# Experts' rows by a scatter into slots, or by a slot-to-row map and a gather per tile

## What is computed

```python
x = x + conv_attention(_ln_c(x), ...)          # 256 tokens per image, 32 key/query channels
t = _to_tokens(x)                              # 2048 tokens of 64 channels
flat = _ln_t(t)
probs = softmax(flat @ router_w.T)             # 8 experts
topk_probs, topk_idx = top_k(probs, 2)         # gates: the two, normalised
h = silu(flat @ w1[e].T) * (flat @ w3[e].T)    # 682 hidden channels
out = sum over the two experts of gate * (h @ w2[e].T)
x = _from_tokens(t + out)
```

## Time and profile before

| | us |
|---|---|
| Three runs | 239.73, 239.23, 238.13 |
| Median | 239.23 |
| The profiled execution | 238.83 |
| Its span, first to last instruction | 237.1 |

### The profile page before, as it was taken

The page is one execution under the profiler, slowest core; times in us unless marked ns, Lnnn a source line. Parts: engine busy times, 40 slices in busy tenths (PEclk is TensorE's granted clock), DMA queues, the critical chain, the costliest instruction groups (busy, mean ns, idle before and its releaser), DMA issues.

```text
span 237.1 us, 4275 instructions
## 1 busy us (share of the span) xinstructions
PE 169.0 (71%) x1424; PEld 136.2 (57%) x1424; DVE 117.4 (50%) x418; ACT 80.2 (34%) x169; POOL 92.1 (39%) x116
## 2 busy tenths in 40 slices
PE   2647789797923000079999999999999999995040
PEld 2536779686813000056787778778777778773010
DVE  3687697579458600025445554455446544552050
ACT  2246344341000000035445544554444544540020
POOL 6232520205777777400044334433443334436300
PEclk9999555555555555559999999999999999999555
DMA  4999500000001000030055534555455500000143
GB/s 138 428 409 411 239 3 0 0 0 7 30 17 33 29 23 29 24 90 0 3 145 170 179 124 132 157 182 144 126 149 178 165 16 13 17 17 17 40 164 80
DMA packets 11928, 24.46 MB, mean 103 GB/s; under 512 B 2435, under 2 KB 6563, under 8 KB 11395
## 3 DMA queue, kind: packets, MB, share of 16 engines
q1 hardware_dynamic: 9410, 21.59, 27.7%
q0 software_dynamic: 2496, 2.59, 3.3%
HBM read 16.74 MB, written 7.44 MB: 102 GB/s over the span
## 4 chain that ended last, share of the span: by engine, by line
issue 37%; POOL 31%; DVE 11%; PE 11%; DMA 5%; ACT 3%; POOLq 1%; SPq 0%; ACTq 0%
POOL ys L323 18%; POOL xs L282 11%; PE bank L787 4%; DVE xn L461 2%; DVE kq_right L493 2%; PE bank L775 2%; DMA y_in<-ys 2%; PE bank L737 1%; POOL rstd L266 1%; DVE parts L452 1%; DVE kq_left L488 1%; DMA x_sb<-x_tok 1%; DMA xs<-rows,pos 1%; DMA ys<-y_out,y_row 1%; DVE neg_max L498 1%
## 5 line engine op out<-in xcount | busy, mean ns | idle before, releaser
L698 DVE TENSOR_TENSOR hid<-bank,act_sb 128x512 f32<-128x512 f32 x69 | 47.6, 690 | 55.9 <-ACT act_sb L415 55.9
L323 POOL DMA_INDIRECT ys<-y_out,y_row x46 | 44.0, 957 | 79.4 <-DVE y_out L705 72.1
L896 PE MATMUL bank<-x_cols,weights 64*128 64x256 f32 x276 | 69.3, 399 | 1.1 <-ACT x_cols L409 0.6
L898 PE MATMUL bank<-x_cols,weights 64*128 64x256 f32 x276 | 69.3, 399 | 0.0
L896 PEld LDWEIGHTS bank<-x_cols,weights 64*128 64x128 f32 x276 | 49.2, 191 | 14.4 <-ACT act_sb L415 4.8
L415 ACT ACTIVATE act_sb<-bank 128x512 f32<-128x512 f32 x69 | 41.3, 598 | 33.3 <-PE bank L896 33.3
L898 PEld LDWEIGHTS bank<-x_cols,weights 64*128 64x128 f32 x276 | 49.3, 191 | 0.0
L913 PE MATMUL bank<-hid,weights 128*64 128x128 f32 x552 | 35.2, 277 | 0.5 <-ACT y_cols L421 0.5
L282 POOL DMA_INDIRECT xs<-rows,pos x32 | 31.2, 976 | 9.7 <-issue 9.7
L913 PEld LDWEIGHTS bank<-hid,weights 128*64 128x64 f32 x552 | 29.7, 137 | 4.3 <-DVE hid L698 3.3
L881 PE MATMUL bank<-ident,x_pairs 128*128 128x128 f32 x46 | 10.4, 309 | 26.4 <-DVE x_pairs L688 26.4
(11 more groups left out here) (123 smaller groups left out, 197.5 us busy)
## 6 DMA issues: line engine op xcount, KB each, us to landing
weights<-experts SPq DMA_DIRECT2D x23, 576.0 KB, 4.1
xs<-zeros SPq DMA_DIRECT2D x4, 1056.0 KB, 8.8
x_in<-xs SPq DMA_DIRECT2D x23, 66.0 KB, 1.9
y_in<-ys SPq DMA_DIRECT2D x4, 256.0 KB, 4.1
ys<-y_out,y_row POOLq DMA_INDIRECT x46, 3.5
xs<-rows,pos POOLq DMA_INDIRECT x32, 2.2
out<-result SPq DMA_DIRECT2D x8, 64.0 KB, 2.1
x_sb<-x_tok SPq DMA_DIRECT2D x1, 384.0 KB, 3.6
```

The source lines that it names most:

```text
L323: nc.gpsimd.indirect_dma_start(ys, bass.IndirectOffsetOnAxis(ap=y_row[:, i, h:h + 1], axis=0), y_out[:, i % RING, h, :], None).then_inc(y_ ...
L698: nc.vector.tensor_tensor(hid[:, g % HRING, :], H3_BANK[g % 3][:], act_sb[:, g % 3, :], ALU.mult).then_inc(hid_done, 1)
L896: first_ = nc.tensor.matmul(H1_BANK[g % 2][:, dst], weights[0:C, i % WSLOTS, at:at + P], x_cols[0:C, i % 2, :], start=True, stop=True)
L898: second_ = nc.tensor.matmul(H3_BANK[g % 3][:, dst], weights[C:P, i % WSLOTS, at:at + P], x_cols[C:P, i % 2, :], start=True, stop=True)
```

## The change

`xs` is now one row of 65 numbers (channels and gate) for each (token, choice) pair, in token order: SP writes it from `rows` in four plain DMAs, and nothing is cleared. Instead of moving rows to slots, the kernel computes the map from slot to pair, `slots`: 128 lanes x 128 columns, slot = 128 x column + lane. For each of the eight (column of tokens, choice) groups j of a block, VectorE makes two one-hot matrices (`lane_hot`, `column_hot`, the second scaled by the pair's number) and TensorE adds their product up in PSUM (`find_slots`); `add_slots` sums over blocks. GpSimd gathers the rows of a tile by this map into `x_in` with two indirect DMAs per tile, five tiles before it scatters that tile's results. For the extras the map's columns are picked by a transpose and a matmul with `select` in the first two tiles of the loop. The ID is no longer read from `x_in`: `y_row` is set by two `copy_predicated` in all instead of 23. `pair_up` now waits for the 32 counts of two gathers.

The diff, cut to its core:

```diff
@@ SP
-            sp.wait_ge(zeros_made, 1)
-            for q in range(NBLK):
-                sp.dma_start(xs[...], zeros[:]).then_inc(xs_cleared, 16)
             for e in range(E):
                 sp.dma_start(weights[:, e, :], experts[e]).then_inc(w_loaded[e], 16)
-            sp.wait_ge(dispatched, 16 * TILES * K_TOP)
-            for i in range(E):
-                sp.dma_start(x_in[:, i, :, :], xs[...]).then_inc(x_in_loaded[i], 16)
+            for k in range(NBLK):
+                sp.wait_ge(tn_ready, k + 1)
+                sp.wait_ge(gates_ready, k + 1)
+                sp.dma_start(xs.rearrange("(p t k) c -> p t k c", t=TILES, k=K_TOP)[:, tiles(k), :, :],
+                             rows[:, tiles(k), :, :]).then_inc(rows_stored, 16)
             sp.wait_ge(table_ready, 1)
             for i in range(E, NT):
...
-                sp.wait_ge(gated, i - WSLOTS + 1)
-                sp.dma_start(x_in[:, s, :, :], xs[bass.ds(r, SLOT), :]...).then_inc(x_in_loaded[s], 16)
                 sp.wait_ge(hid_used, STEPS * (i - WSLOTS + 1))
@@ GpSimd
-            def scatter_rows(k):
...
+            def gather_rows(i):
+                s = i % WSLOTS
+                if i >= WSLOTS:
+                    pool.wait_ge(gated, i - WSLOTS + 1)
+                if i == E:
+                    pool.wait_ge(extra_rows_ready, 1)
+                for h in range(HALVES):
+                    at = CAP // P * i + h
+                    index = slots_i[:, at:at + 1] if i < E else extra_rows[:, i - E, h:h + 1]
+                    nc.gpsimd.indirect_dma_start(x_in[:, s, h, :], None, xs,
+                                                 bass.IndirectOffsetOnAxis(ap=index, axis=0)
+                                                 ).then_inc(x_in_loaded[s], 16)
...
+            for k in range(NBLK):
+                inverse_deviation(1, k)
+            pool.wait_ge(rows_stored, 16 * NBLK)
+            pool.wait_ge(slots_added, NBLK)
+            for i in range(AHEAD):
+                gather_rows(i)
             for i in range(NT):
+                if i + AHEAD < NT:
+                    gather_rows(i + AHEAD)
+                scatter_results(i)
@@ ACT, expert loop
+                if i == 1:
+                    act.wait_ge(slots_turned, 1)
+                    nc.scalar.copy(slots_t[:], R_BANK[:, 0:P]).then_inc(slots_t_ready, 1)
@@ VectorE, positions(k)
-                    nc.vector.tensor_reduce(pos[:, k, :]..., place[:], AX.X, ALU.add).then_inc(pos_ready, 1)
+                    chain(nc.vector.tensor_reduce(pos[:]..., place[:], AX.X, ALU.add))
+                chain(nc.vector.tensor_scalar(low_bits[:], pos[:], P - 1, None, ALU.bitwise_and))
+                nc.vector.tensor_copy(pos_lane[:], low_bits[:]).then_inc(dve_step, 1)
+                chain(nc.vector.tensor_tensor(pos_column[:], pos[:], low_bits[:], ALU.subtract))
+                if k >= 2:
+                    dve.wait_ge(slots_done, k - 1)
+                for j in range(TPB * K_TOP):
+                    nc.vector.tensor_scalar(lane_hot[:, k % 2, j, :], lane[:], pos_lane[:, j:j + 1], None, ALU.is_equal)
+                    t = TPB * k + j // K_TOP
+                    nc.vector.tensor_scalar(column_hot[:, k % 2, j, :], column[:], pos_column[:, j:j + 1],
+                                            row_id[:, t, j % K_TOP:j % K_TOP + 1], ALU.is_equal, ALU.mult
+                                            ).then_inc(hot_ready, 1)
+            def add_slots(k):
+                dve.wait_ge(slots_done, k + 1)
...
+                    nc.vector.tensor_tensor(slots[:], slots[:], found, ALU.add).then_inc(slots_added, 1)
+                else:
+                    nc.vector.tensor_tensor(slots_i[:], slots[:], found, ALU.add).then_inc(slots_added, 1)
+                    nc.vector.tensor_tensor(slots[:], slots[:], found, ALU.add).then_inc(slots_added, 1)
@@ VectorE, order
                     weigh(k - 2)
+                    if k >= 3:
+                        add_slots(k - 3)
                     positions(k - 2)
...
             choose(NBLK - 2)
+            add_slots(NBLK - 3)
             weigh(NBLK - 2)
             positions(NBLK - 2)
             choose(NBLK - 1)
             weigh(NBLK - 1)
+            add_slots(NBLK - 2)
             positions(NBLK - 1)
+            add_slots(NBLK - 1)
             tile_table()
+            nc.vector.copy_predicated(y_row[:, 0:E, :], keep[:, 0:E, :], slots_i[:]...).then_inc(y_row_ready, 1)
@@ VectorE, expert loop
-                nc.vector.copy_predicated(y_row[:, i, :], keep[:, i, :], x_in[:, slot, :, ID].bitcast(I32)
-                                          ).then_inc(y_row_ready, 1)
+                if i == 1:
+                    result_rows_of_extras()
@@ TensorE
             def rank(k):
...
-                    pe.wait_ge(rank_read, k)
+                    pe.wait_ge(slots_added, k)
+            def find_slots(k):
+                for j in range(TPB * K_TOP):
+                    pe.wait_ge(hot_ready, TPB * K_TOP * k + j + 1)
...
+                    ins = nc.tensor.matmul(K_BANK[:, 0:COLS], lane_hot[:, k % 2, j, :], column_hot[:, k % 2, j, :],
+                                           start=(j == 0), stop=(j == TPB * K_TOP - 1))
+                ins.then_inc(slots_done, 1)
...
                     similarity(BPB * (k + 1) + 1)
+                if k >= 3:
+                    find_slots(k - 3)
                 attend(BPB * k)
...
             transpose_t(NBLK - 1)
+            find_slots(NBLK - 3)
             rank(NBLK - 2)
             route(NBLK - 1)
+            find_slots(NBLK - 2)
             rank(NBLK - 1)
+            find_slots(NBLK - 1)
...
+                if i == 0:
+                    pe.wait_ge(slots_added, NBLK + 1)
+                    nc.tensor.transpose(R_BANK[:, 0:P], slots[:], ident[:]).then_inc(slots_turned, 1)
+                if i == 1:
+                    pe.wait_ge(slots_t_ready, 1)
+                    pe.wait_ge(select_ready, 1)
+                    nc.tensor.matmul(R_BANK[:, P:P + NX * HALVES], slots_t[:], select[:]..., start=True, stop=True
+                                     ).then_inc(selected, 1)
```

More of the change, by code:

```diff
@@ L271, in count_up, with scatter_results @@
                                allow_small_or_imprecise_dtypes=True).then_inc(tables_made, 1)
[L273 to L284 removed]
+            def gather_rows(i):
[10 more added lines that the diff above has]
+                                                 ).then_inc(x_in_loaded[s], 16)
+            def scatter_results(i):
+                pool.wait_ge(gated, i + 1)
+                pool.wait_ge(y_row_ready, 1 if i < E else 2)
+                for h in range(HALVES):
+                    nc.gpsimd.indirect_dma_start(
+                        ys, bass.IndirectOffsetOnAxis(ap=y_row[:, i, h:h + 1], axis=0),
+                        y_out[:, i % RING, h, :], None).then_inc(y_scattered[i % RING], 16)
             inverse_deviation(0, 0)
@@ L571, in positions @@
                 dve.wait_ge(rank_read, k + 1)
-                with nc.allow_low_precision(reason="row numbers: whole and below 2^24"):
-                    nc.vector.tensor_reduce(pos[:, k, :].rearrange("p (t c) -> p t c", c=K_TOP), place[:], AX.X,
-                                            ALU.add).then_inc(pos_ready, 1)
+                with nc.allow_low_precision(reason="slot numbers: whole and below 2^24"):
+                    chain(nc.vector.tensor_reduce(pos[:].rearrange("p (t c) -> p t c", c=K_TOP), place[:], AX.X,
+                                                  ALU.add))
+                chain(nc.vector.tensor_scalar(low_bits[:], pos[:], P - 1, None, ALU.bitwise_and))
+                nc.vector.tensor_copy(pos_lane[:], low_bits[:]).then_inc(dve_step, 1)
+                steps[0] += 1
+                chain(nc.vector.tensor_tensor(pos_column[:], pos[:], low_bits[:], ALU.subtract))
[9 more added lines that the diff above has]
+                dve.wait_ge(slots_done, k + 1)
+                found = K_BANK[:, 0:COLS]
+                if k >= 1:
+                    dve.wait_ge(slots_added, k)
+                if k == 0:
+                    nc.vector.tensor_copy(slots[:], found).then_inc(slots_added, 1)
+                elif k < NBLK - 1:
+                    nc.vector.tensor_tensor(slots[:], slots[:], found, ALU.add).then_inc(slots_added, 1)
+                else:
+                    nc.vector.tensor_tensor(slots_i[:], slots[:], found, ALU.add).then_inc(slots_added, 1)
+                    nc.vector.tensor_tensor(slots[:], slots[:], found, ALU.add).then_inc(slots_added, 1)
             def occupancy(part):
@@ L932, in _ @@
                     turn_x(i + 1)
+                if i == 0:
[4 more added lines that the diff above has]
+                    pe.wait_ge(select_ready, 1)
+                    nc.tensor.matmul(R_BANK[:, P:P + NX * HALVES], slots_t[:], select[:].rearrange("p i h -> p (i h)"),
+                                     start=True, stop=True).then_inc(selected, 1)
```

115 lines of the change are left out of this document (57 added, 58 removed).

## The result

| | us |
|---|---|
| Before, beside the changed kernel | 239.44 (238.13 to 239.73) |
| The changed kernel | 295.41 (294.08 to 296.26) |
| Ratio | 1.237, 95% interval 1.232 to 1.243 |
| Its profiled execution | 295.41, span 293.7 |

The forecast was 238.4 in a range of 235.4 to 243.0. It is wrong by 57 us. Both times are told, and both profiles are read.

The account below looks back on a forecast made before the run. Bounds: GpSimd's scatters before the loop, TensorE in the expert loop. 238.83 - 2.3 (earlier tile start) + 0.5 (TensorE's added steps) + 1.0 (loop stall) = 238.0, and 0.4 to the median: 238.4 us, range 235.4 to 243.0.

Parts of the forecast that it names:

- One-hots, 14.7 us for 64: Before the loop, VectorE makes 64 one-hots at 0.20 and 0.26 us, a pair 0.46, in all 14.7 us.
- The estimate of 0.127: Skill page's price of one one-hot on VectorE, 8.1 us for all 64; the forecast set it aside for measured rows.
- Map ready at 93.9, pair_up(0) at 99.2: Before the loop, VectorE's chain ends the map at 93.9; tiles start at 99.2 instead of 101.53: -2.3 us.
- Gathers ahead of the loop are hidden: GpSimd's first gathers run beside the table from 93.9 and land at 97.4, before pair_up(0) at 99.2: no cost.
- TensorE's +0.5: In the loop, TensorE gets one transpose (0.27) and one matmul of 30 columns (some 0.2): +0.5 us.
- The loop's +1.0: In the loop, four GpSimd DMAs a tile take 5.04 against 4.82 us; TensorE's stall from this lag: +1.0 us.
- a late gated passes into later gathers: In the loop, GpSimd's wait for a late gated delays the gathers two tiles on; no size in the sum.
- the 4.9 that bounded L: L is a gather's landing time in the loop, 2.1 to 4.9 us, median 3.5; 4.9 makes the stall 2.5.
- the prediction's own formula: TensorE's loop loss: 16 x 0.22 + L + 3.78 - 7.27 - 2.4, with L a gather's landing time; 1.1 us at 3.5.
- GpSimd sets the loop's pace: Rival: x_pairs copies slow GpSimd by 0.2 a tile above 5.04, loop stall 4.3, total 241.7 to 243.1; chance 0.24, at 242.4.
- The lock rule: Skill rule: each x_pairs copy shuts GpSimd out of writing descriptors, 5.33 us a tile, loop stall 5.7, total 243.1.
- no difference: Outcome that the change can't be told from the kernel before, within about 1% (236.8 to 241.6 us); chance 0.40.

Follow-up runs that it names:

- chip 4: The changed kernel with no edit, run again on another chip than the first runs, 10 executions: 240.88 us, against 238.8 for the kernel before.
- the first run: The changed kernel with no edit, in its first measurement, chip not known: 295.41 us, against 239.44 for the kernel before.
- the kernels made from it: The kernel before with dummy gathers, dummy scatters or a memset added behind the scatters of all or some tiles: 238.59 to 312.62 us.
- pauses: The changed kernel with memsets on GpSimd as pauses: one behind each pair of indirect DMAs 279.65 us, one behind each four 272.12 us.
- plain stores: The changed kernel with each tile's results stored by two plain DMAs instead of two scatters, output not right: 232.37 us.
- dummies in tiles 0 to 5: The kernel before with two more full scatters to a spare tensor behind each of tiles 0 to 5 only: 238.59 us.
- chips 12 and 6: Kernel before plus one scatter 240.84, a memset 242.33, two 16-row scatters 246.15; two full scatters in tiles 0 to 5 238.59, 17 to 22 246.75 us.
- chips 0, 8 and 13: Kernel before plus two DMAs a tile: gathers 300.5, full scatters 308.3 and again 307.15, scatters of 64 rows 285.05, of 96 rows 312.62 us.
- eight runs in two groups: Variants of both kernels with added, shortened, spaced or replaced GpSimd DMAs: four on chip 12, 232.37 to 246.15 us, four on chip 8, 272.12 to 312.62 us.

## Why the prediction was right or wrong

**Without the late signals** (chip 4) it can be judged by its own steps. The page of this profile, against the earlier trace rows, and the stage of the earlier trace rows:

```profile
PE   2647789787734924599999996989998999997031
...
POOL 3232620201020003771677775777777777564500
```

```profile
118.00:214.00 96.00, 91.14 (x958) 71.29 (x956) 43.70 (x92) 42.84 (x93) 69.89 (x71) 1.00 0.40 106
```

- **One-hots, 14.7 us for 64: right.** 0.20 and 0.26, as read from L473 and from the price of one scalar. The estimate of 0.127 (the Trainium skill, VectorE: DVE Perf Modes, the section on the TRN2 errata) would have made them 6.6 us too short.
- **Map ready at 93.9, pair_up(0) at 99.2: right.** The first x_pairs starts at 97.16 on chip 4 and 98.09 in the first run, but not all of this is the change. The attention ahead of it, in which no instruction was edited, ends at another time in each execution, and TensorE's granted clock is high at other times (in before it stays low from 24.6 us on, on chip 4 it is high again from 48.5 to 55.3): place(0) starts at 53.2 to 55.9 us in the 20 traces, with either dispatch (before 55.48, here 53.77, in the first run 54.43). From place(0) to the first x_pairs it is 46.05 us before (46.0 to 46.2 in the kernels made from it) and now 43.39 (43.66 in the first run), where the forecast says 99.2 - 55.48 = 43.7. The gain is 2.4 to 2.7 us, and 2.3 was said.
- **Gathers ahead of the loop are hidden: right**, since they start 4 us before x_pairs. The second x_pairs does wait 2.1 us for its gathers, which was not foreseen, at no cost that shows: the first y_out is 16.55 us behind the first x_pairs, and 15.9 to 16.9 in before and in the kernels made from it. In that spread TensorE's +0.5 can't be seen either.
- **The loop's +1.0: the step that failed, twice.** Here its size is wrong. From the first x_pairs to the last y_out the loop takes 122.57 us (97.16 to 219.73) against 115.87 before (101.53 to 217.40): +6.7, where 0.5 + 1.0 was said. Of the 6.7, 6.1 lie between the first y_out and the last (106.02 against 99.92). GpSimd needs 5.16 a tile, and not 5.04. Its timeline:

```profile
114.27 1.01 POOL L298 DMA_INDIRECT ys<-y_out,y_row  x1 [6.06 <-DVE y_out L764]
115.59 0.98 POOL L298 DMA_INDIRECT ys<-y_out,y_row  x1 [0.30 <-issue]
116.87 0.99 POOL L290 DMA_INDIRECT x_in<-xs,slots_i  x1 [0.30 <-issue]
118.17 0.96 POOL L290 DMA_INDIRECT x_in<-xs,slots_i  x1 [0.30 <-issue]
119.44 1.00 POOL L298 DMA_INDIRECT ys<-y_out,y_row  x1 [0.30 <-issue]
```

The chain of waits goes through one gather (start, us), and VectorE's waits from 118 to 214 us (total, times, longest) say how x_pairs fared:

```profile
139.22 5.76 DMA x_in<-xs,extra_rows
145.39 0.68 DVE hid L757
```

```profile
DVE x_pairs L749 <- DMA x_in<-xs,extra_rows: 34.7, 15, 4.1
```

Each of the four took about 0.03 more than the 0.96 of the earlier trace rows, which over 16 tiles is a lag of 16 x 0.34 = 5.4 instead of 3.5. But GpSimd's lag came to 7.9 us: tile 16's scatter starts at 199.25, 84.98 behind the first (77.12 before). The other 2.4 are waits of GpSimd itself. The prediction names them (a late gated passes into later gathers) but has them at nothing in its sum. The largest comes from one gather that was 5.76 us on its way, beyond the 4.9 that bounded L. x_pairs waited 4.1 us for it, y_out stands behind x_pairs in VectorE's list, and GpSimd, whose next scatter needs that y_out, stood idle for 1.78 us instead of 0.30, and issued all of its later gathers 1.5 us later:

```profile
145.01 0.46 DVE L749 COPY x_pairs<-x_in 128x256 f32<-128x256 f32 x1 [4.12 <-DMA x_in<-xs,extra_rows]
...
146.58 0.28 DVE L764 TENSOR_TENSOR y_out<-bank,x_in 128x128 f32<-128x128 f32 x1
```

```profile
147.14 1.00 POOL L298 DMA_INDIRECT ys<-y_out,y_row  x1 [1.78 <-DVE y_out L764]
```

The last gather was on its way for 3.87 us (issued at 203.23, x_pairs at 207.10), not far above the median of 3.5 in the earlier trace rows. With these the prediction's own formula (the lag, plus the way of a gather, less what the schedule leaves for it, less the slack) gives 7.9 + 3.9 - 3.5 - 2.4 = 5.9 us, against 6.1 measured: the formula holds, and the terms that it had too small are GpSimd's time per tile (1.9 us of the lag) and GpSimd's own waits (2.4), at nothing without a reason. So it was the rival "GpSimd sets the loop's pace" that came true, and not the forecast. Its mechanism is right; its 0.2 a tile above 5.04 was 0.12, and its stall of 4.3 was 5.9, since it left out the same waits. The lock rule that was weighed with it (the Trainium skill, SBUF — State Buffer, "SBUF: two separate sides") would give 5.33 a tile; the trace says 5.16.

In the profiled execution (239.9 us, 1.1 above that of before) the parts are: attention -1.7, the stage with the map -2.7, the loop +6.7, and -1.3 behind the last y_out (18.4 us instead of 19.7), which the prediction had at nothing. In the six traces of the new dispatch with neither pauses nor plain stores this tail is 18.3 to 18.5 us, in before and with dummies in tiles 0 to 5 it is 19.6 to 19.7; no run shows why. Between the medians the difference is 2.1 us (1.7 with 240.5). The 240.88 lies within the range, and no difference, the likeliest of the three outcomes, is what was found there; but this is in part luck, since a loop that was 5.2 us dearer than said was offset by a shorter tail and, in the execution that was profiled, by an early attention.

**With the late signals** no step of the sum says anything. The sum asked of each wait on the path who was busy, and took for granted that a semaphore follows its instruction at once, since 0.01 to 0.05 us is all that the trace of before shows. The trace could not have warned. It does hold a stretch of the right kind, GpSimd's first scatters beside a busy TensorE (56 to 66 us, TensorE busy for 8.12 of 10 us), and all signals are on time there, as they are in the runs on chips 12 and 6; on chips 0, 8 and 13 the same instructions show one that is 2.3 us late. What it doesn't hold is four indirect DMAs a tile beside the full TensorE of the loop, where the lateness lies on the path. A range made from such rows can't hold 295. The text priced GpSimd's own time beyond 4.82 us and put the effect of four DMAs on the other engines' signals at nothing, without saying that no row showed that state. That is the step that failed here: in its place the runs show signals up to 7.4 us late, three tiles in 23.5 us, and no cause behind it that could be named.

**What the change is worth.** With three indirect DMAs a tile instead of four the changed kernel takes 234.81 us, 1.6% less than before, and with two 232.37. Neither computes the result (half of the rows, or the place of the results, is wrong), so no kernel better than before was found; but both take 99.9 us from the first y_out to the last, as before, where the changed kernel takes 106.0. The gain ahead of the loop is real, and the fourth DMA gives it back even without late signals.

## What to carry to other kernels

A queue that is filled to more than its period (here 4 x 1.29 against 4.82 us) never catches up, so whatever it is itself made to wait stays in its lag: ask which of its transfers, when late, holds back the work that the queue waits for (here 2.4 us on top of 5.4). If a slow-down is a circle of waits in which no engine is busy, compare the times of the semaphore updates with the ends of the instructions that send them. And before explaining a large loss by the kernel, run the unchanged kernel on a second chip: here eight runs in two groups, each on one chip, gave a neat threshold between three and four DMAs that isn't there.

## What the hardware showed that was not expected

- TensorE's semaphore updates can come several us behind their matmuls (7.4 us in the changed kernel) while indirect DMAs are issued beside it: the changed kernel takes 295 to 299 us so, and 241 without. VectorE's came up to 1.0 us late beside the old dispatch's scatters. In the groups where this happened it struck every kernel with four a tile (272 to 313 us), and none in the others. The Trainium skill says that "DMA never contends with a compute engine" (SBUF — State Buffer, "Who interferes with whom"). That section is about ports and doesn't speak of signals. Whoever reads it as "indirect DMAs never delay TensorE" is misled in these runs, though they can't say whether the DMAs or their recording do it.
- An indirect DMA of 16 rows takes GpSimd 0.85 us, of 64 rows 0.90, of 128 rows 0.96: nearly all of it is paid for each instruction and not for each row.
- A standstill is paid for again in TensorE's clock. In the period shown, after TensorE had stood nearly still since 176, its granted clock was at the lower level (0.5 of 2.4 GHz) for 6.8 us (179.2 to 186.0), some 4 of them with TensorE at work again (6.00 of 6.00 us from 182).
